# Sixteen row slots instead of nine in the gathers of two graph convolutions

## The chip, the cores and the metric

The kernel runs on one core of a Trainium2 chip. The time is the device time of one execution in microseconds (us). Before the change the median of three timed runs is 11113.99 us (11105.82 to 11126.48).

## The reference, cut to what matters

The kernel computes four layers of a graph network over 6250 nodes of 128 features and 106250 edges (100000 edges and one loop for each node), sorted by destination. The last layer is two graph convolutions, and the change touches these alone:

```
def _graph_conv(h, src, dst, Wr, br, Ws, ew=None):
    m = h[src]
    if ew is not None:
        m = m * ew[:, None]
    agg = jax.ops.segment_sum(m, dst, num_segments=h.shape[0])
    return agg @ Wr + br + h @ Ws
h = relu(_graph_conv(x, src, dst, Wr0, br0, Ws0, edge_weight))
h = relu(_graph_conv(h, src, dst, Wr1, br1, Ws1))
return _layernorm(x + h)
```

## The kernel before, in words

The kernel is a sequence of stages with a barrier of all engines between any two. First the edges are sorted by source and by destination; then come the attention layers, each of which gathers node rows by edge; then `gather_conv` runs twice (lines 2650 and 2653), once from `x_table` to `conv_table` ("conv0") and once from `conv_table` to the output ("conv1").

The edges, padded, are cut into tiles of 128 and the tiles into `R` = 126 groups of `G` = 7. Only 879 of the 882 tiles hold edges. For each group the engines of `gather_conv` do the following, in program order on each engine, with semaphores between them:

- GpSimd (line 1426 on) issues one indirect DMA a tile. It fetches the 128 rows (512 bytes each) that the tile's edges name from the table in HBM into `rows[:, g % deep, t % G, :]`. `deep` is the number of row slots, 9 before the change, each of seven tiles. Each slot has a semaphore `fetched[g % deep]`. Before the first gather of a group `g >= deep` GpSimd waits until the group that used the slot before has been multiplied.
- VectorE builds `weighted_hot(g + 1)` (line 1460): for each tile a 128x128 matrix that has an edge's weight in the column of its destination, counted from the tile's first destination. There are `near` = 3 buffers. Then, in `add(g)`, it waits for `summed >= g + 1` and adds the group's seven 128x128 products from PSUM to `acc` and `odd` by turns (line 1473), at an offset that it loads from a table.
- TensorE's `sums(g)` waits for the hot matrices, for the slot's rows and for a free PSUM buffer (`near` = 3 of these too). It then multiplies rows by hot matrix, seven products that appear in the profile as 14 weight loads and 14 matmuls since they are f32 (line 1526), and the last one increments `summed`. Every nine groups it also transposes four blocks of the layer's own input and multiplies them by `Ws` (lines 1534, 1542, 1543); ScalarE copies these out of PSUM (lines 1388, 1392). Once the sums of a block of nodes are complete, which is the case only in the last groups (118 on), it is multiplied by `Wr` (lines 1555, 1556) and finished on VectorE and ScalarE.
- ScalarE in conv0 also issues a small DMA a group (line 1419), which nothing on the other engines waits for within the stage.

The wait that the change moves, and the only one on GpSimd in this stage:

```
for g in range(R):
    if g >= deep:
        pool.wait_ge(summed, g - deep + 1)
    for t in range(g * G, min(g * G + G, TD)):
        pool.indirect_dma_start(
            rows[:, g % deep, t % G, :], None, table, ...).then_inc(fetched[g % deep], 16)
```

The attention stages (`attend`, gathers at line 1644) have the same loop with `RING` = 19 slots, and there the slot is freed by a later step (`msg_ready`, or `summed`).

Of the kernel before, what the change touches and what calls it, by code (L numbers as in the profile page):

```python
# [1340 lines left out]
                    pipelined(pe, R // SLOTS, SLOTS, differences, sums)  # L1341


def gather_conv(nc, c, o, name, acc, alpha, table, k, unit=None, deep=9, near=3):

# [1219 lines left out]
def gnn_kernel(nc, out, x_in, src, dst, length, edge_weight, real, p):  # L2567
    with ExitStack() as keep:
# [18 lines left out]
        with ExitStack() as first_layer:  # L2587
# [4 lines left out]
            with ExitStack() as sums:  # L2592
                scores = sums.enter_context(nc.sbuf_tensor("scores", [P, T * H0], F32))
                with ExitStack() as edges:
# [53 lines left out]
        h_nodes = sb("h_nodes", [P, NB, D])  # L2648
        unit = sb("unit", [P, T])
        gather_conv(nc, c, by_dst, "conv0", acc, by_dst.weight, x_table,  # L2650
                    {"own": x, "wr": conv_w[:, 0], "ws": conv_w[:, 1], "b": conv_b[0:1, 0], "nodes": h_nodes,
                     "table": conv_table}, unit)
        gather_conv(nc, c, by_dst, "conv1", acc, unit, conv_table,
                    {"own": h_nodes, "wr": conv_w[:, 2], "ws": conv_w[:, 3], "b": conv_b[0:1, 1], "nodes": h_nodes,
                     "residual": x, "out": out})
# [43 lines left out]
```

## Time and profile before

| | |
|---|---|
| Median of the timed runs | 11113.99 us |
| The profiled execution's own time | 11120.83 us |
| Its span | 11119.1 us |
| GpSimd busy | 6028.3 us (54%) |
| TensorE matmuls busy | 5741.4 us (52%) |
| VectorE busy | 5139.9 us (46%) |
| ScalarE busy | 2208.4 us (20%) |
| Mean granted TensorE clock | 0.638 of full speed |
| Gathers of conv0 | 8492.9 to 9745.0 us |
| Gathers of conv1 | 9790.4 to 11041.8 us |

PE is TensorE, PEld its weight loads, DVE is VectorE, ACT is ScalarE, POOL is GpSimd, SP is SyncE. In a timeline each row gives the start in us from the span's beginning, the duration, the engine, the line, the instruction with what it writes and reads, how many such instructions were merged into the row, and in brackets how long the engine was idle before it and what ended that idle time. That last name is inferred; where it is a DMA that had long landed, another semaphore ended the wait. "issue" is time in which the engine waited for nothing that the profile shows. No engine is busy for much more than half of the span, so the time is set by waits between them, stage by stage.

### The profile page before, as it was taken

How to read it: one execution, taken by the hardware profiler on the slowest of the kernel's cores; microseconds unless marked ns; L12 is line 12 of the kernel's file. 1: busy time of each engine (PE TensorE's matmuls, PEld its weight loads, DVE VectorE, ACT ScalarE, POOL GpSimd, SP SyncE). 2: the span in 40 equal slices, each digit the busy share in tenths (PEclk: the TensorE clock that was granted, in tenths of full speed). 3: DMA queues.
4: the chain of work that ended last, by engine and by line, in shares of the span. 5: the costliest groups of instructions: out<-in, count | busy, mean ns of one | idle time of the engine just before them, and what ended most of it. 6: DMA issues, size and time to landing. Idle time of an engine off the chain costs nothing. (4 is left out here: it accounts for less than half of the span.)

```text
span 11119.1 us, 123007 instructions
## 1 busy us (share of the span) xinstructions
PE 5741.4 (52%) x32437; PEld 5060.6 (46%) x32437; DVE 5139.9 (46%) x16751; ACT 2208.4 (20%) x4780; POOL 6028.3 (54%) x6231
## 2 busy tenths in 40 slices
PE   6656654566635666653555554466562333333333
PEld 5545544566634555543455543355452333233323
DVE  7555543333356666662555554244454333333334
ACT  0111111111114444431433433211111000000000
POOL 2555554555534666644544442465543666656664
PEclk8555556777765666666777776555555556666656
DMA  1000004555533444423333333233321222221111
GB/s 28 9 9 10 9 1 116 159 160 159 162 85 92 105 105 105 101 84 86 95 92 93 95 90 40 58 66 65 65 52 32 47 47 47 47 51 46 47 46 46
DMA packets 991728, 792.42 MB, mean 71 GB/s; under 512 B 425142, under 2 KB 866874, under 8 KB 991024
## 3 DMA queue, kind: packets, MB, share of 16 engines
q1 hardware_dynamic: 535572, 373.20, 13.4%
q0 software_dynamic: 211104, 354.07, 13.3%
q10 hardware_dynamic: 244600, 60.13, 2.5%
q8 instruction: 160, 2.62, 0.1%
q14 instruction: 292, 2.39, 0.1%
HBM read 692.16 MB, written 94.60 MB: 71 GB/s over the span
## 5 line engine op out<-in xcount | busy, mean ns | idle before, releaser
L1526 PE MATMUL conv_ps_sum<-conv_hot,conv_rows 128*128 128x128 f32 x3528 | 729.2, 382 | 1523.2 <-DVE conv_hot L1460 1034.7
L1526 PEld LDWEIGHTS conv_ps_sum<-conv_hot,conv_rows 128*128 128x128 f32 x3528 | 665.5, 285 | 1585.6 <-DVE conv_hot L1460 1119.6
L515 POOL DMA_INDIRECT payload_src<-load_src_pay,load_src_at_i x879 | 897.7, 1021 | 804.7 <-DVE load_src_at_i L479 543.2
L1644 POOL DMA_INDIRECT attend_rows<-xl_table,dst_other x879 | 829.7, 944 | 871.3 <-DVE attend_msg L1876 592.4
L1051 POOL DMA_INDIRECT scores_rows<-kv_table,scores_idx x882 | 834.0, 946 | 661.6 <-DVE scores_prod L1125 330.5
L1431 POOL DMA_INDIRECT conv_rows<-x_table,dst_other x879 | 840.6, 956 | 626.7 <-issue 252.8
L636 POOL DMA_INDIRECT payload_dst<-place_dst_pay,place_dst_at_i x879 | 855.8, 974 | 589.5 <-DVE place_dst_at_i L777 314.5
L1644 POOL DMA_INDIRECT attend_rows<-h_table,dst_other x879 | 830.7, 945 | 619.7 <-issue 236.0
L1431 POOL DMA_INDIRECT conv_rows<-conv_table,dst_other x879 | 840.0, 956 | 456.7 <-issue 254.9
L1473 DVE TENSOR_TENSOR acc<-acc,conv_ps_sum 128x128 f32 x1008 | 291.4, 289 | 1687.7 <-DMA x_table<-x_nodes 771.4
L1704 PE MATMUL attend_ps_x<-attend_win,attend_hot_t 128*128 128x136 f32 (+1 forms) x3528 | 754.1, 321 | 408.9 <-issue 226.9
L1704 PEld LDWEIGHTS attend_ps_x<-attend_win,attend_hot_t 128*128 128x128 f32 x3528 | 658.0, 257 | 464.3 <-issue 437.5
L1721 PE MATMUL attend_ps_sum<-attend_hot,attend_rows 128*128 128x128 f32 x1764 | 417.3, 429 | 505.3 <-DVE acc L1896 465.3
L1085 PE MATMUL scores_ps_len<-const_ident,scores_length 128*128 128x128 f32 x1764 | 383.9, 403 | 518.5 <-ACT scores_hidden L1030 295.6
L1721 PEld LDWEIGHTS attend_ps_sum<-attend_hot,attend_rows 128*128 128x128 f32 x1764 | 385.4, 330 | 521.9 <-issue 521.9
L1896 DVE TENSOR_TENSOR acc<-acc,attend_ps_sum 128x128 f32 x1764 | 505.5, 287 | 234.9 <-remote 67.6
L1721 PE MATMUL attend_ps_sum<-attend_hot,attend_msg 128*128 128x128 f32 x1764 | 343.2, 360 | 519.3 <-DVE acc L1896 415.9
L1085 PEld LDWEIGHTS scores_ps_len<-const_ident,scores_length 128*128 128x128 f32 x1764 | 353.8, 305 | 537.4 <-issue 537.4
L1721 PEld LDWEIGHTS attend_ps_sum<-attend_hot,attend_msg 128*128 128x128 f32 x1764 | 303.3, 261 | 560.2 <-issue 513.3
L1790 ACT ACTIVATE attend_hot_t<-attend_rel_all,const_minus_lane 128x896 f32<-128x896 bf16 x252 | 261.5, 1038 | 1303.7 <-remote 724.8
L1841 DVE SCALAR_TENSOR_TENSOR attend_mix<-attend_ps_x,att_wide 128x408 f32<-128x408 f32 x378 | 181.7, 484 | 722.6 <-remote 597.2
L691 PE MATMUL place_dst_ps_look<-place_dst_tab,place_dst_lo_t 128*128 128x50 f32 x1764 | 335.8, 367 | 304.8 <-DVE place_dst_picked L771 282.7
(442 smaller groups left out, 14393.1 us busy)
## 6 DMA issues: line engine op xcount, KB each, us to landing
attend_win<-xr_table SPq DMA_DIRECT2D x882, 68.0 KB
scores_win<-q_table ACTq DMA_DIRECT2D x882, 64.0 KB
spill<-scores_rows SPq DMA_DIRECT2D x126, 448.0 KB
place_dst_key_all<-key_rows_dst SPq DMA_DIRECT2D x126, 448.0 KB
place_dst_rows<-spill SPq DMA_DIRECT2D x126, 448.0 KB
attend_rel_all<-rel_flat_dst SPq DMA_DIRECT2D x252, 224.0 KB
place_dst_low_all<-low_rows_dst SPq DMA_DIRECT2D x126, 224.0 KB
scores_rows<-kv_table,scores_idx POOLq DMA_INDIRECT x882
```

What stands on the lines that cost most here:

```text
L515: pool.indirect_dma_start(o.payload, bass.IndirectOffsetOnAxis(ap=at_i[:, t:t + 1].bitcast(U32), axis=0), pay[:, t, :], None).then_inc(sca ...
L636: pool.indirect_dma_start(o.payload, bass.IndirectOffsetOnAxis(ap=at_i[:, t:t + 1].bitcast(U32), axis=0), pay[:, t, :], None).then_inc(sca ...
L691: mm = pe.matmul(ps_look[:, j, 0:HB], lo_t[:, g % 2, j, :], tab[:, g % 2, j, :], start=True, stop=True)
L1051: pool.indirect_dma_start(rows[:, s, j, :], None, table, bass.IndirectOffsetOnAxis(ap=idx[:, s, j:j + 1].bitcast(U32), axis=0)).then_inc(g ...
L1085: mm = pe.matmul(ps_len[:, j, :], length[:, s, j:j + 1].to_broadcast([P, P]), c.ident[:], start=True, stop=True)
L1431: pool.indirect_dma_start(rows[:, g % deep, t % G, :], None, table, bass.IndirectOffsetOnAxis(ap=o.other[:, t:t + 1].bitcast(U32), axis=0) ...
L1473: dve.tensor_tensor(at, at, ps_sum[:, n, j, :], ALU.add).then_inc(added, 1)
L1526: mm = pe.matmul(ps_sum[:, g % near, j, :], rows[:, g % deep, j, :], hot[:, g % near, j, :], start=True, stop=True)
L1644: pool.indirect_dma_start(rows[:, g % RING, t % G, :], None, table, bass.IndirectOffsetOnAxis(ap=o.other[:, t:t + 1].bitcast(U32), axis=0) ...
L1704: mm = pe.matmul(ps_x[:, bank, at:at + window_w], hot_t[:, g % 2, j, :], win[:, g % 3, j, :], start=True, stop=not two_sided)
L1721: mm = pe.matmul(ps_sum[:, j, :], what, hot[:, g % 2, j, :], start=True, stop=True)
L1896: dve.tensor_tensor(at, at, ps_sum[:, j, :], ALU.add).then_inc(added, 1)
```

## The change

One default value is changed. Both calls use it, so both convolutions have sixteen slots of seven tiles. The tile `rows` grows from 9 x 7 x 128 f32 (32,256 bytes a partition) to 16 x 7 x 128 f32 (57,344 bytes), and there are sixteen `fetched` semaphores instead of nine. `near`, the number of hot matrices and of PSUM buffers, stays 3.

```
-def gather_conv(nc, c, o, name, acc, alpha, table, k, unit=None, deep=9, near=3):
+def gather_conv(nc, c, o, name, acc, alpha, table, k, unit=None, deep=16, near=3):
```

## Rows read from the trace of the kernel before

**Rows 1.** The gathers' own line: durations, and what GpSimd's idle time before them ended with.

```profile
L1431 POOL DMA_INDIRECT conv_rows<-x_table,dst_other x879: 938/944/7480, 8492.9 to 9745.0; - x176
L1431 POOL DMA_INDIRECT conv_rows<-conv_table,dst_other x879: 938/944/7480, 9790.4 to 11041.8; - x176
...
  DMA x_table<-x_nodes: 155.7, 51
  DMA attend_rows<-h_table,dst_other: 153.3, 54
  PE conv_ps_sum L1526: 8.2, 4
```

**Rows 2.** Timeline of GpSimd, first convolution: start, duration, instruction, idle before.

```profile
8492.92 0.94 POOL L1431 DMA_INDIRECT conv_rows<-x_table,dst_other  x1 [214.15 <-POOLq L78]
...
8515.83 0.94 POOL L1431 DMA_INDIRECT conv_rows<-x_table,dst_other  x1 [0.30 <-issue]
...
8594.52 0.94 POOL L1431 DMA_INDIRECT conv_rows<-x_table,dst_other  x1 [0.30 <-issue]
8602.42 0.94 POOL L1431 DMA_INDIRECT conv_rows<-x_table,dst_other  x1 [6.95 <-DMA x_table<-x_nodes]
...
9104.77 0.94 POOL L1431 DMA_INDIRECT conv_rows<-x_table,dst_other  x1 [3.86 <-DMA x_table<-x_nodes]
...
9134.65 0.94 POOL L1431 DMA_INDIRECT conv_rows<-x_table,dst_other  x1 [3.86 <-DMA x_table<-x_nodes]
...
9745.04 0.94 POOL L1431 DMA_INDIRECT conv_rows<-x_table,dst_other  x1 [0.30 <-issue]
```

**Rows 3.** Timeline of TensorE, the second, third and fourth groups of the first convolution.

```profile
8518.44 3.33 PE L1526 MATMUL conv_ps_sum<-conv_hot,conv_rows 128*128 128x128 f32 x14 [4.84 <-DMA conv_rows<-x_table,dst_other]
...
8527.27 3.23 PE L1526 MATMUL conv_ps_sum<-conv_hot,conv_rows 128*128 128x128 f32 x14
...
8551.07 0.37 PE L1526 MATMUL conv_ps_sum<-conv_hot,conv_rows 128*128 128x128 f32 x1 [2.43 <-issue]
8553.87 0.37 PE L1526 MATMUL conv_ps_sum<-conv_hot,conv_rows 128*128 128x128 f32 x1 [2.43 <-issue]
```

**Rows 4.** Timeline of VectorE, the first additions of some groups of the first convolution.

```profile
8602.28 0.29 DVE L1473 TENSOR_TENSOR acc<-acc,conv_ps_sum 128x128 f32 x1 [75.76 <-DMA x_table<-x_nodes]
...
8616.38 0.29 DVE L1473 TENSOR_TENSOR acc<-acc,conv_ps_sum 128x128 f32 x1 [10.76 <-DMA x_table<-x_nodes]
...
9104.63 0.29 DVE L1473 TENSOR_TENSOR acc<-acc,conv_ps_sum 128x128 f32 x1 [19.10 <-DMA x_table<-x_nodes]
...
9134.51 0.29 DVE L1473 TENSOR_TENSOR acc<-acc,conv_ps_sum 128x128 f32 x1 [17.75 <-DMA x_table<-x_nodes]
...
9748.22 0.29 DVE L1473 TENSOR_TENSOR acc<-acc,conv_ps_sum 128x128 f32 x1 [3.79 <-PE conv_ps_sum L1526]
...
9751.47 0.28 DVE L1473 TENSOR_TENSOR acc<-acc,conv_ps_sum 128x128 f32 x1
...
9779.39 0.29 DVE L1473 TENSOR_TENSOR acc<-acc,conv_ps_sum 128x128 f32 x1 [0.97 <-PE conv_ps_sum L1526]
```

**Rows 5.** Timeline of ScalarE, then two stretches of the first convolution (columns as headed).

```profile
8563.68 0.59 ACT L1392 COPY h_nodes<-conv_ps_n 128x512 f32<-128x512 f32 x1 [49.46 <-DMA attend_rows<-h_table,dst_other]
...
core 0: us, PE busy (x) PEld busy (x) DVE busy (x) ACT busy (x) POOL busy (x), PEclk, DMA share, GB/s
8493.00:8596.00 103.00, 20.37 (x76) 17.26 (x76) 21.05 (x44) 1.17 (x2) 79.30 (x77) 0.53 0.20 49
9104.00:9134.00 30.00, 15.41 (x57) 12.60 (x57) 10.05 (x42) 0.58 (x1) 19.92 (x21) 0.56 0.22 47
```

**Rows 6.** Two stretches of the first attention stage, and GpSimd's timeline in it.

```profile
5045.00:5095.00 50.00, 4.33 (x16) 3.72 (x16) 2.03 (x3) 2.08 (x2) 37.74 (x40) 0.50 0.31 70
5195.00:5245.00 50.00, 33.34 (x243) 31.53 (x242) 32.97 (x78) 21.43 (x27) 0.00 (x0) 0.91 0.60 139
...
5254.43 0.94 POOL L1644 DMA_INDIRECT attend_rows<-xl_table,dst_other  x1 [93.54 <-DVE attend_msg L1876]
```

## The prediction

> **What bounds the kernel now.** I read the page's head first, then its costliest groups, then the gathers' own line, the engines' timelines at the start, middle and end of the first convolution, and a table of stretches. The change touches only the two convolution stages at the end, each with 879 gathers. The reader is to see two things in the gathers' rows. One gather occupies GpSimd for 944 ns, and the next starts 0.30 us later, so the steady pace is 1.25 us a gather and 8.75 us a group of seven (8492.92 to 8594.52 is 76 steps, one of which is the 7.48 us of the longest gather). At that pace 879 gathers are 1098 us, but the first convolution's run from 8492.9 to 9745.0, which is 1252 us; the second's is the same to a microsecond [rows 1, 2]. The difference is GpSimd standing still: 155.7 + 153.3 + 8.2 = 317 us over both stages, in 109 waits [rows 1]. The first two names in those rows are DMAs that had long ended; by the code the only thing a gather waits for here is `summed` of the group that held its slot, so these are waits for a free slot, and they are what more slots could take away.
>
> Who is late? Not the gathered data. Group 1's last gather starts at 8515.83 and its matmuls start at 8518.44: 2.6 us from issue to use, against nine slots that cover 79 us [rows 2, 3]. The late one is the consumer, in a peculiar way. The third group's matmuls stand at 8527.27 and take 3.23 us, yet VectorE, which waits for nothing but their semaphore, starts that group's additions at 8602.28, after 75.76 us idle [rows 3, 4]. Meanwhile TensorE's rows crawl: the last two matmuls of the fourth group start at 8551.07 and 8553.87, 2.80 us apart with one weight load between them, so 1.40 us an instruction, where the group before took 3.23 / 14 = 0.23 us for such a pair [rows 3]. ScalarE gets the semaphore of the products that ended at 8527 only at 8563.68 [rows 5]. From there to VectorE's release at 8602.28 is 38.6 us, and a group is 28 TensorE instructions: 28 x 1.40 = 39.2 us. So while GpSimd issues gathers without a break, TensorE's work goes through at about 39 us a group, far slower than GpSimd's 8.75 us, and GpSimd runs to the end of its slots: 77 gathers, eleven groups, before its first stop [rows 2, 5].
>
> In the middle the same thing repeats with a period of some 30 us. GpSimd stands still for 3.86 us (to 9104.77), then again to 9134.65; between them are 21 gathers, three groups. VectorE's additions come in bursts right at those moments (9104.63 after 19.10 us idle, 9134.51 after 17.75 us idle) [rows 2, 4, 5]. The pause of GpSimd is what lets the consumer catch up by three groups, and the slot it hands back lets GpSimd go on. Over the stage the consumer goes from group 2 (8602.28) to group 118 (9748.22): 1145.9 / 116 = 9.88 us a group. Once GpSimd is done (9746) and quiet, it takes 3.25 us for an ordinary group (9748.22 to 9751.47) [rows 2, 4].
>
> **The change, part by part.** *Instructions.* None is added or removed: 879 gathers, 126 groups, the same matmuls. Seven more semaphores and 25,088 bytes more a partition cost nothing that a row shows; I put them at 0, with the stage's set-up (the 5 us or so before its first memset) as the upper end.
>
> *The start of a convolution.* GpSimd needs `summed` of group g-16 instead of g-9. Groups 0 to 15 wait for nothing, 16, 17 and 18 need the first, second and third sum, which are there by 8602. Group 19 needs the fourth. By the crawl of 39 us a group this comes at 8602 + 39 = 8641, and the fifth at 8680, and GpSimd reaches groups 19 and 20 at 8493 + 6.5 (the long gather) + 19 x 8.75 = 8666 and 8674. So the first stop moves from before group 11 to before group 19 or 20. The price is the shift, less what the crawl got done in it: 8 x 8.75 - 1 x 9.88 = 60.1 us, or 9 x 8.75 - 2 x 9.88 = 59.0 us. I take 59.5 us. The bounds: 0 if the crawl is not caused by GpSimd's run and the consumer would have gone free at 8602 anyway; 79 us if nothing at all goes through in the longer run.
>
> *The middle.* The cycle of three groups and a pause depends on where the consumer stands relative to its own semaphores, not on how far ahead the slot is that it frees: the data has landed 2.6 us after issue in either case. So 9.88 us a group stays. This is the term I can prove least.
>
> *The end.* When the last gather is issued, the consumer is behind by up to sixteen groups instead of nine. Seven more groups are therefore consumed in quiet, at 3.25 to 3.4 us and not 9.88: (9.88 - 3.35) x 7 = 45.7 us gained. The lower bound is 38 us, at the pace of the last seven groups, which also carry the closing products: (9779.39 - 9748.22) / 7 = 4.45 us [rows 4].
>
> *Sum.* 59.5 - 45.7 = +13.8 us a convolution, +28 us for two (ends of the terms: 2 x (0 - 45.7) = -91 to 2 x (79 - 38) = +82). On the profiled execution's own 11120.8 us (span 11119.1) this is 11149. The median of the timed runs is 6.8 us lower, so 11142.
>
> There is a second case of a long run with more slots in this trace: the first attention stage has 19, and it is the same form of gather. It starts at 4995; in 5045 to 5095 GpSimd issues 40 gathers while TensorE gets 16 matmuls done; GpSimd then stands still for 93.54 us until 5254.43, and in 5195 to 5245, with no gather, TensorE does 243 [rows 6]. A longer ring there bought a longer starved run and a longer stop.
>
> **The rule that speaks the other way.** The trace shows the same gap of 3.9 us over and over on GpSimd [rows 2]. The Trainium skill, page "Perfetto Trace Analysis", section "Optimization Strategy", says that consistent bubbles on the engine that should be saturated can mean that there isn't enough SBUF for the next tile (number of buffers). By that rule the change is the cure, and the time is that of rival 2 below; the trace agrees that the wait is for a slot, but not that the slots are few against the 2.6 us of a landing.
>
> **Rivals.** (1) *The start does not get dearer.* If the crawl ends by itself at about 8602, and the pause of GpSimd has only the same moment, the 59.5 us disappear and the 45.7 us at the end stay: 11120.8 - 91 = 11029, or 11023 on the median. For it: ScalarE's semaphore came at 8563.68 and VectorE's at 8602.28, inside or just after an unbroken run, and 39.2 us predicts the second without any pause. Against it: the same arithmetic gives the next group another 39 us, and the additions of group 3 came at 8616.38, right after a second pause [rows 4]. It decides from the point at which less than 45.7 of the 59.5 us are lost.
> (2) *The slots do what they are for.* Without any stop, 317 us go; if sixteen groups are left at the end, 7 x 3.35 x 2 = 47 us come back: 11120.8 - 317 + 47 = 10851. Against it is the consumer's 9.88 us against GpSimd's 8.75.
> (3) *It cancels.* The start costs 40 to 50 us, as when the longer run lets one or two groups more slip through: 11100 to 11130, no change.
>
> **How the numbers follow.** A measurement of this kernel can tell about 0.2% (22 us) from no change. Forecast, the start outweighs the end: 0.50, with its own range 11125 to 11175. Rival 3: 0.26. Rival 1: 0.19. Rival 2: 0.05. The forecast case lies mostly above 11136, a tenth of it below, and rival 3 has a small upper tail that makes up for this, so slower is 0.50, same 0.26, faster 0.24. The range reaches from 11040, into the milder half of rival 1, up to 11180.
>
> **What would show it.** In the changed profile: the first row of a gather with an idle time of several us in the first convolution comes after 133 to 140 gathers instead of 77, and VectorE's idle row of 76 us is followed by rows of 20 to 39 us before that stop. In the middle the pauses keep a period near 30 us with 21 gathers. The gathers' waits sum to some 295 us instead of 317, and from the last gather to the last addition it is 55 to 60 us instead of 34. Wrong is the forecast if the additions after 8602 go on at 10 us a group while GpSimd still has free slots, or if the pauses vanish.

## The result, and the profile after

The changed kernel takes 11140.14 us (median of 9 runs, 11126.24 to 11170.75) where the kernel before takes 11108.96 us on the same chip (9 runs, 11098.13 to 11140.3). The ratio is 1.0034 with an interval of 1.0022 to 1.0046: slower by 31 us. The forecast was 11142 us, slower by 28. The profiled execution of the changed kernel has 11149.92 us (span 11148.2).

Times within a convolution are given below from its first gather. This table is worked out from the timelines of both kernels. "Sum of group n" is the first of VectorE's additions of that group, and the tail is from the start of the last gather to the first addition of the last group, 125.

| us from the first gather | before, conv. 1 | after, conv. 1 | before, conv. 2 | after, conv. 2 |
|---|---|---|---|---|
| sum of group 2 | 109.4 | 106.0 | 109.4 | 108.7 |
| sum of group 3 | 123.5 | 145.2 | 123.5 | 147.9 |
| sum of group 4 | 126.7 | 184.4 | 126.7 | 187.1 |
| sum of group 5 | 131.6 | 211.7 | 130.8 | 211.6 |
| sum of group 10 | 193.2 | 255.0 | 193.1 | 254.6 |
| sum of group 60 | 678.9 | 747.2 | 691.1 | 746.8 |
| sum of group 100 | 1083.1 | 1147.1 | 1089.4 | 1151.4 |
| start of the last gather | 1252.1 | 1250.7 | 1251.4 | 1251.4 |
| sum of group 125 | 1286.5 | 1306.3 | 1310.2 | 1331.3 |
| tail | 34.3 | 55.6 | 58.7 | 80.0 |

The gathers' own line after the change, against [rows 1]:

```profile
L1431 POOL DMA_INDIRECT conv_rows<-x_table,dst_other x879: 942/947/7470, 8480.9 to 9731.6; - x176
L1431 POOL DMA_INDIRECT conv_rows<-conv_table,dst_other x879: 942/947/7470, 9798.2 to 11049.6; - x176
...
  DMA attend_rows<-h_table,dst_other: 152.9, 46
  DMA attend_rel<-rel_rows_dst: 152.5, 42
```

From the first gather to the last it is 1250.7 and 1251.4 us, as before (1252.1 and 1251.4). GpSimd still stands still for 152.9 + 152.5 = 305 us, and not 317. The waits are fewer and longer. GpSimd's timeline, first convolution, against [rows 2]:

```profile
8665.42 0.95 POOL L1431 DMA_INDIRECT conv_rows<-x_table,dst_other  x1 [2.86 <-DMA attend_rows<-h_table,dst_other]
...
8692.73 0.95 POOL L1431 DMA_INDIRECT conv_rows<-x_table,dst_other  x1 [18.80 <-DMA attend_rows<-h_table,dst_other]
...
9081.17 0.95 POOL L1431 DMA_INDIRECT conv_rows<-x_table,dst_other  x1 [4.18 <-DMA attend_rows<-h_table,dst_other]
...
9111.22 0.95 POOL L1431 DMA_INDIRECT conv_rows<-x_table,dst_other  x1 [4.01 <-DMA attend_rows<-h_table,dst_other]
...
9731.59 0.95 POOL L1431 DMA_INDIRECT conv_rows<-x_table,dst_other  x1 [0.30 <-issue]
```

The first stop is now before gather 141, the first of group 20. Before, it was before gather 78. The second, one group later, is 18.80 us. In the middle the old cycle is back: 30.05 us between two stops of some 4 us. VectorE's additions at the start, against [rows 4]:

```profile
8586.88 0.29 DVE L1473 TENSOR_TENSOR acc<-acc,conv_ps_sum 128x128 f32 x1 [73.48 <-DMA attend_rows<-h_table,dst_other]
...
8626.08 0.29 DVE L1473 TENSOR_TENSOR acc<-acc,conv_ps_sum 128x128 f32 x1 [35.85 <-DMA attend_rows<-h_table,dst_other]
...
8665.28 0.29 DVE L1473 TENSOR_TENSOR acc<-acc,conv_ps_sum 128x128 f32 x1 [35.85 <-DMA attend_rows<-h_table,dst_other]
...
8692.59 0.29 DVE L1473 TENSOR_TENSOR acc<-acc,conv_ps_sum 128x128 f32 x1 [23.96 <-DMA attend_rows<-h_table,dst_other]
```

These are the sums of groups 2, 3, 4 and 5. The first three are 39.20 us apart, twice. The kernel before had only the first of these idle rows: its next sum came 14.10 us later, during GpSimd's second stop, and the one after it 3.3 us after that. TensorE's timeline in the same time shows what crawls:

```profile
8590.28 3.36 PE L1526 MATMUL conv_ps_sum<-conv_hot,conv_rows 128*128 128x128 f32 x14 [52.14 <-issue]
8629.48 3.36 PE L1526 MATMUL conv_ps_sum<-conv_hot,conv_rows 128*128 128x128 f32 x14 [35.84 <-DVE conv_hot L1460]
```

The row at 8590.28 is the fifth lot of fourteen, group 4. Once it is started it takes 3.36 us, against 3.33 and 3.23 us in [rows 3], and is done at 8593.64; VectorE adds its products at 8665.28, 72 us later. So the multiplications themselves are not slow here. What comes late is the semaphore that tells of them, and TensorE then idles because VectorE can't hand it the next hot matrices and PSUM buffer. "Crawl" below means this: the sums of one group after another reach VectorE some 39 us apart. ScalarE's first copy against [rows 5], and four stretches (start and end, length, then busy time and count of TensorE's products, its weight loads, VectorE, ScalarE and GpSimd, the granted clock, the DMA share, GB/s):

```profile
8547.58 0.59 ACT L1392 COPY h_nodes<-conv_ps_n 128x512 f32<-128x512 f32 x1 [45.05 <-issue]
```

```profile
8481.00:8584.00 103.00, 20.40 (x76) 17.21 (x76) 21.05 (x44) 1.17 (x2) 79.58 (x77) 0.53 0.20 49
8584.00:8660.00 76.00, 6.72 (x28) 6.13 (x28) 6.69 (x28) 0.00 (x0) 57.65 (x61) 0.52 0.21 53
8481.00:9732.00 1251.00, 402.32 (x1818) 353.16 (x1818) 383.86 (x1569) 14.82 (x26) 841.62 (x879) 0.59 0.22 47
9732.00:9794.00 62.00, 49.51 (x396) 47.70 (x396) 54.34 (x211) 7.75 (x13) 0.54 (x1) 0.93 0.29 50
```

The first 103 us are those of before to the last count (76 products, 77 gathers). Then come 76 us of the longer run that the further slots bought: 61 gathers issued, and 28 products done. In the 62 us after the last gather there are 396 products. The same two stretches of the kernel before, on GpSimd's stretch and on what followed it:

```profile
8493.00:9746.00 1253.00, 423.86 (x1927) 373.03 (x1928) 408.04 (x1668) 14.79 (x26) 840.47 (x879) 0.60 0.23 47
9746.00:9786.00 40.00, 34.92 (x289) 34.43 (x288) 31.05 (x111) 7.56 (x12) 0.00 (x0) 0.88 0.34 75
```

In the same time of GpSimd, TensorE got 1927 - 1818 = 109 products fewer done. They moved behind the last gather. That is the effect: the producer takes as long as before, and the consumer is further behind when it ends.

To the start of the last group's additions this is 1306.3 - 1286.5 = 19.8 us in the first convolution and 1331.3 - 1310.2 = 21.1 us in the second, 41 us together. The profiled executions differ by 29 us only, because the stages ahead of the first convolution, which the change doesn't touch, took 12.0 us less in the changed kernel's (its first gather is at 8480.9, and was at 8492.9).

### The profile page after: what moved, and what is told of

It is laid out like the page before. It is cut to its first block and busy times, and to the rows that moved or that the text cites. A ratio compares the mean times of both kernels' runs of the same rounds, so it can differ in the third digit from the quotient of the medians.

```text
span 11148.2 us, 123007 instructions
## 1 busy us (share of the span) xinstructions
PE 5717.2 (51%) x32437; PEld 5039.4 (45%) x32437; DVE 5139.5 (46%) x16751; ACT 2211.5 (20%) x4780; POOL 6046.2 (54%) x6231
```

## The experiments

Two theories stood against each other. **Theory A** is that of the prediction: while GpSimd issues gathers without a break, TensorE's work goes through at 39 us a group, more slots mean a longer unbroken run, and the catching up at the end gives back only a part. **Theory B** is plain buffering: fewer slots make GpSimd stop longer, so fewer than nine must be slower. A third view was tested beside them, that only the start of a stage crawls.

The kernel before was run beside each experiment, and it turned out that the chips are of two kinds. On three of those with experiments ("e5", "e10" and "e12"), and in the runs of the result, whose chip is one of these or a fourth, it takes 11106 to 11121 us. On three others (the rest of the experiments) it takes 8840 to 8845 us, and there TensorE never crawls. That was not known when the first four were forecast, and none of the outcomes forecast for those four under either theory came. Nine runs in all fell on chips without the crawl and tell something other than what they were meant for.

**The changed kernel again.** No edit: `deep=16` as in the change.

> The changed kernel itself, beside the kernel before on one chip. In the four comparisons made so far here (three, five, late sixteen slots, and the pause) the kernel before took 8840 us and not 11114, and GpSimd never waited for a slot. If the kernel before is again at 8840, theory A expects no difference (ratio 1.000, within 0.002): without TensorE's crawl the consumer keeps up with 8.8 us a group, no slot is ever waited for, and sixteen slots stand as empty as nine. If it is again near 11110, theory A expects the ratio on record, 1.003, with the first stop of GpSimd before group 20. Rival: sixteen slots cost something by themselves (memory placement, semaphores), and the ratio is 1.003 at 8840 too.

Measured: 11163.02 us against 11105.91; the ratio is 1.005, from 1.0034 to 1.0065. The sums come at 110.8, 150.0, 188.5 and 211.7 us in the first convolution, the last gather starts at 1249.8 and the tail is 55.3 us. VectorE's timeline:

```profile
8648.69 0.29 DVE L1473 TENSOR_TENSOR acc<-acc,conv_ps_sum 128x128 f32 x1 [35.86 <-DMA attend_rows<-h_table,dst_other]
...
8687.19 0.29 DVE L1473 TENSOR_TENSOR acc<-acc,conv_ps_sum 128x128 f32 x1 [35.16 <-DMA attend_rows<-h_table,dst_other]
```

The slowdown (forecast 1.003) and its shape come again in a second set of runs, with the first stop before group 20; the step here is 39.2 and then 38.5 us.

**Fewer slots, and more of them later, on chips without the crawl.** Three and five slots change one number:

```diff
-def gather_conv(nc, c, o, name, acc, alpha, table, k, unit=None, deep=9, near=3):
+def gather_conv(nc, c, o, name, acc, alpha, table, k, unit=None, deep=3, near=3):
```

```diff
-def gather_conv(nc, c, o, name, acc, alpha, table, k, unit=None, deep=9, near=3):
+def gather_conv(nc, c, o, name, acc, alpha, table, k, unit=None, deep=5, near=3):
```

> Three row slots instead of nine in both convolutions, nothing else. Theory A (GpSimd's unbroken run starves TensorE, which gets a group through in 39.2 us while it lasts; what the run costs at the start is partly paid back at the end): the first stop comes before group 5 and not 11, some 52 us earlier, and at the end six groups fewer are consumed in quiet, 6 x 6.6 = 40 us lost. So about 12 us less a convolution, 25 us less in all than before (ratio 0.998). TensorE's crawl at the start shrinks from 76 us to about 25. Theory B (slots are plain buffering): with 26 us of slots GpSimd stops more often and longer, its waits grow over the 317 us of before, and the kernel is 50 us or more slower.

> Five row slots instead of nine. Theory A: first stop before group 7, 35 us earlier; four groups fewer in quiet at the end, 26 us lost; 9 us less a convolution, 17 us less in all (ratio 0.9985). Theory B: slower than before, between the three slots and the nine.

> Three row slots again, to be read if the kernel before is near 11110 here, that is where TensorE crawls. Theory A (an unbroken run of GpSimd starves TensorE, 39.2 us a group; slots let the run at the start grow and are paid back in part at the end): sizes from nine against sixteen are 66 us lost at the start and 48 us won back at the end for seven slots, so six slots fewer save 57 and cost 41 us: 16 us less a convolution, 25 to 32 us less in all (ratio 0.9975). The first stop of GpSimd comes before group 5. Theory B (plain buffering): the slots cover 26 us against a consumer that is served in bursts of 30 us, so GpSimd's stops grow well over 159 us a convolution and the kernel is 50 us or more slower. If the kernel before is at 8840: same.

The late widening has the changed kernel's sixteen slots, but GpSimd stays within nine groups of the consumer up to group 59:

```diff
-                    if g >= deep:
-                        pool.wait_ge(summed, g - deep + 1)
+                    back = 9 if g < 60 else deep
+                    if g >= back:
+                        pool.wait_ge(summed, g - back + 1)
```

> Sixteen slots are there, but up to group 59 GpSimd waits as with nine, and from group 60 as with sixteen. Theory A: the starved run doesn't belong to the start but to any unbroken run of GpSimd; it comes at group 60, seven groups and more without a stop, costs about the same 60 to 66 us there and pays back 46 to 48 us at the end, so the time is that of sixteen slots from the start, 28 to 38 us over before. Rival (only the cold start of the stage starves TensorE): nothing is lost at group 60 and the end pays back 46 us a convolution, so 90 us less than before.

> Sixteen slots, used as nine up to group 59, where the kernel before is near 11110. Theory A: an unbroken run of nine or more groups from group 60 with the third, fourth, fifth sum 39.2 us apart, a loss of 60 to 66 us there and 48 us won back at the end: 28 to 57 us over before in all (ratio 1.0025 to 1.005), as with sixteen from the start. Rival (only the stage's start can starve): 90 us less than before (0.992). If the kernel before is at 8840: same.

Measured: three slots 8836.36 us against 8839.9 (ratio 0.9999, 0.999 to 1.0008), and again 8845.67 against 8845.17 (1.0002, 0.9993 to 1.0011); five slots 8837.73 against 8839.9 (1.0000, 0.9991 to 1.0009); the late widening 8835.57 against 8839.9 (0.9999, 0.999 to 1.0008), and again 8843.92 against 8845.17 (0.9997, 0.9988 to 1.0006). Five runs of three kernels, and none can be told from nine slots. The gathers' own line with three slots says why:

```profile
L1431 POOL DMA_INDIRECT conv_rows<-x_table,dst_other x879: 940/944/7477, 6574.1 to 7678.9; - x176
L1431 POOL DMA_INDIRECT conv_rows<-conv_table,dst_other x879: 938/944/7486, 7696.2 to 8801.3; - x176
its engine sat idle before it (us, times) until:
  issue: 535.1, 1756
  POOLq L78: 212.4, 2
```

There is no wait for a slot at all, with three slots. The last gather starts 1104.8 us after the first, and 878 x 1.25 + 6.5 for the one long gather is 1104. So nothing that the kernel computes needs nine slots, let alone sixteen. One stretch of the first convolution and one of the first attention stage, and VectorE's first addition of group 2, of the same kernel:

```profile
6574.00:6677.00 103.00, 39.64 (x164) 35.67 (x164) 48.72 (x156) 1.76 (x3) 79.60 (x77) 0.58 0.25 49
4057.00:4107.00 50.00, 26.99 (x167) 25.84 (x166) 18.91 (x35) 12.50 (x12) 37.81 (x41) 0.81 0.59 147
```

```profile
6611.85 0.29 DVE L1473 TENSOR_TENSOR acc<-acc,conv_ps_sum 128x128 f32 x1 [5.08 <-PE conv_ps_sum L1526]
```

77 gathers in 103 us, as in [rows 5], but 164 products beside them where the crawling chip did 76. In the attention stage it is 167 products beside 41 gathers in 50 us, against 16 beside 40 in [rows 6]. The third sum comes at 37.7 us and not at 109.4. GpSimd's pace and the 49 GB/s of the DMAs are the same on both kinds. The gathers' unbroken issue is thus not enough to make TensorE crawl; something that differs between the chips belongs to it. These five runs don't tell A from B: on these chips neither has anything to act on.

**A pause of GpSimd ahead of every third group.** If GpSimd's silence is what lets TensorE go on, short early pauses should pay for themselves. GpSimd waits until the gathers of the group before have landed:

```diff
+                    if g and g % 3 == 0:
+                        pool.wait_ge(fetched[(g - 1) % deep], landed(g - 1, deep))
```

> Nine slots as before, and before every third group GpSimd waits until its own last gathers have landed (about 2.2 us after their issue). Theory A, with the pause as what frees TensorE: the crawl never builds up or ends at each pause, the consumer keeps up, and GpSimd's own pace sets the time: 1098 us of issue + 42 pauses of 1.5 to 2.5 us = 1160 to 1200 us instead of 1252, with a short tail; 60 to 100 us less a convolution, 120 to 200 us less in all. If a landing is too short a pause to free TensorE (the stops in the trace lasted 3.9 us): no better than before, or up to 2 x 42 x 1.6 = 130 us slower. Theory B (TensorE's crawl has nothing to do with GpSimd's run): GpSimd has slack of 154 us a convolution, so the pauses change nothing: same as before.

> Nine slots, and before every third group GpSimd waits for its own last landing; where the kernel before took 8840 us this pause was 2.36 us each and the kernel 167 us slower. Where the kernel before is near 11110: if a silence of 2.4 us frees TensorE (theory A with a short release), the crawl never lasts over 26 us, the consumer keeps up, and 60 to 100 us a convolution are saved, ratio 0.982 to 0.99. If TensorE needs the 3.9 us of silence that ended each crawl in the trace, the pauses add to or replace the stops: 0.998 to 1.01. If the crawl has nothing to do with GpSimd's issuing, the pauses eat only its slack of 159 us a convolution: 1.000.

> The pause before every third group once more, to be read if the kernel before is near 11110. If a silence of 2.4 us frees TensorE (theory A with a short release): 60 to 100 us saved a convolution, ratio 0.982 to 0.99. If TensorE needs some 3.9 us of silence, as ended each crawl in the trace: 0.998 to 1.01. If the crawl has nothing to do with GpSimd's issuing, the pauses (42 of 2.36 us, 99 us a convolution) only eat its slack of 159 us: 1.000. If the kernel before is at 8840: 1.019 as twice before.

> The pause before every third group, to be read if the kernel before is near 11110. GpSimd's stops so far come every three or four groups and last 3.9 us whatever the slots, as if 26 us of issue and 3.9 us of silence were one cycle. If a silence of 2.4 us, put there every 26 us, frees TensorE as well: no further stops, GpSimd is done after 1098 + 42 x 2.4 = 1199 us instead of 1252, and the consumer is at most four groups behind: 60 to 100 us saved a convolution, ratio 0.982 to 0.99. If it takes the 3.9 us: the pauses are too short, stops come on top of them, 0.998 to 1.01. If the crawl has nothing to do with GpSimd's issuing: 1.000. If the kernel before is near 8840: 1.019.

Measured: 9007.04 us against 8839.9 (1.0196, 1.0182 to 1.021), 9012.93 against 8845.17 (1.0192, 1.0178 to 1.0206), 9004.08 against 8843.22 (1.0185, 1.0168 to 1.0202) and 9011.63 against 8844.36 (1.0185, 1.0167 to 1.0203). It fell on a chip without the crawl each time, four times in all. The first of them is slower than every outcome forecast for it. From it the price was known, and 1.019 was forecast for such a chip in two of the later ones. What it shows is the price of the pauses where they bring nothing, in the waits of the gathers' line:

```profile
  DMA conv_rows<-conv_table,dst_other: 94.6, 41
  DMA conv_rows<-x_table,dst_other: 94.5, 40
```

94.5 / 40 = 2.36 us each, where a gap of 0.30 us would have stood anyway: 41 x 2.06 = 84 us a convolution, and twice that is about the 167 us of the medians. Whether 2.4 us of silence frees TensorE on a crawling chip was not seen and stays open.

**The late widening on a crawling chip.** The same edit as above. It tells whether the loss belongs to the start of a stage or to any unbroken run.

> Sixteen slots used as nine up to group 59, once more, to be read if the kernel before is near 11110. Theory A: GpSimd runs on from group 60 for nine groups or more without a stop, and in that run the sums come 39.2 us apart; 60 to 66 us lost there a convolution, 48 us won back at the end, 28 to 57 us over before (ratio 1.0025 to 1.005). Rival (only a stage's start starves TensorE): 90 us less than before (0.992). If the kernel before is near 8840: 1.000.

Measured: 11151.14 us against 11109.12, ratio 1.0035 (1.002 to 1.0049). The start is that of nine slots: the sums of groups 2 to 5 come at 110.1, 123.5, 126.8 and 130.9 us, where the kernel before has 109.4, 123.5, 126.7 and 131.6. The loss comes where the slots come. GpSimd's timeline around group 60; the rows between the first two all have 0.30 us of idle time:

```profile
9067.52 0.95 POOL L1432 DMA_INDIRECT conv_rows<-x_table,dst_other  x1 [3.98 <-DMA attend_rows<-h_table,dst_other]
...
9177.85 0.94 POOL L1432 DMA_INDIRECT conv_rows<-x_table,dst_other  x1 [5.47 <-DMA attend_rows<-h_table,dst_other]
...
9195.46 0.95 POOL L1432 DMA_INDIRECT conv_rows<-x_table,dst_other  x1 [9.15 <-DMA attend_rows<-h_table,dst_other]
```

VectorE's in the same time, and its first addition of the last group:

```profile
9100.70 0.29 DVE L1474 TENSOR_TENSOR acc<-acc,conv_ps_sum 128x128 f32 x1 [21.19 <-DMA attend_rows<-h_table,dst_other]
...
9139.20 0.29 DVE L1474 TENSOR_TENSOR acc<-acc,conv_ps_sum 128x128 f32 x1 [35.15 <-DMA attend_rows<-h_table,dst_other]
...
9177.71 0.29 DVE L1474 TENSOR_TENSOR acc<-acc,conv_ps_sum 128x128 f32 x1 [35.17 <-DMA attend_rows<-h_table,dst_other]
...
9791.03 0.29 DVE L1474 TENSOR_TENSOR acc<-acc,conv_ps_sum 128x128 f32 x1 [0.97 <-PE conv_ps_sum L1527]
```

At the widening GpSimd runs for 110.3 us and twelve groups without a stop, and the sums come 38.5 us apart as at a start with sixteen slots. From group 60 on the kernel stands where the changed one stands: the sum of group 60 at 748.3 us (747.2), of group 100 at 1146.6 (1147.1), of group 125 at 1305.3 (1306.3). The loss belongs to the longer unbroken run wherever it falls, not to the start of the stage. Nor does it come from the larger tile or the seven further semaphores as such: they are there from the start in this kernel, and up to group 59 it keeps the pace of nine slots.

**Five slots on a crawling chip.** If A holds, the opposite edit must win: GpSimd stops earlier, and less is left for the tail.

> Five row slots once more, to be read if the kernel before is near 11110. In the profiles of nine, sixteen and late sixteen slots GpSimd's own stretch from first to last gather is 1250 to 1252 us whatever the slots, and only the tail after it changes: 34 us with nine, 55 to 57 us with sixteen. Theory A: GpSimd's stretch stays 1250 us (first stop before group 7, cycle of 30 us unchanged), and the tail is four groups shorter, some 4 x 2.9 = 12 us; 8 to 13 us saved a convolution, 16 to 26 us in all (ratio 0.9977 to 0.9986). Theory B (plain buffering): GpSimd's stretch grows by 10 us or more. If the kernel before is near 8840: 1.000.

Measured: 11099.45 us against 11121.01, ratio 0.9977 (0.9962 to 0.9991): faster than nine slots, and so than both kernels of this case. The gathers' own line:

```profile
L1431 POOL DMA_INDIRECT conv_rows<-x_table,dst_other x879: 938/944/7476, 8493.4 to 9743.7; - x176
L1431 POOL DMA_INDIRECT conv_rows<-conv_table,dst_other x879: 938/944/7478, 9781.3 to 11033.6; - x176
...
  DMA attend_rows<-h_table,dst_other: 314.4, 134
```

Its GpSimd at the start of the first convolution:

```profile
8568.09 0.94 POOL L1431 DMA_INDIRECT conv_rows<-x_table,dst_other  x1 [7.18 <-DMA attend_rows<-h_table,dst_other]
...
8597.86 0.94 POOL L1431 DMA_INDIRECT conv_rows<-x_table,dst_other  x1 [3.83 <-DMA attend_rows<-h_table,dst_other]
```

And VectorE at the first of these, and at the last group:

```profile
8567.96 0.29 DVE L1473 TENSOR_TENSOR acc<-acc,conv_ps_sum 128x128 f32 x1 [40.70 <-DMA attend_rows<-h_table,dst_other]
...
9770.31 0.29 DVE L1473 TENSOR_TENSOR acc<-acc,conv_ps_sum 128x128 f32 x1 [0.97 <-PE conv_ps_sum L1526]
```

The first row is the sum of group 2, at 74.5 us. With nine and with sixteen slots it came at 106 to 111 us in every trace of a crawling chip. What the edit changes up to there is that GpSimd fell silent, at 8560.9, and 7 us later the sum was there. This is the direct evidence that GpSimd's silence lets TensorE's work through.

The slots side by side, first convolution on crawling chips, from the timelines:

| slots | first gather to last | stops over 0.6 us, sum | sum of group 100 | tail | sum of group 125 |
|---|---|---|---|---|---|
| 5 | 1250.3 | 159.3 | 1050.0 | 26.6 | 1276.9 |
| 9 | 1252.1 | 159.2 | 1083.1 | 34.3 | 1286.5 |
| 16 | 1250.7 | 154.8 | 1147.1 | 55.6 | 1306.3 |
| 16 from group 60 | 1250.0 | 155.9 | 1146.6 | 55.4 | 1305.3 |

The first two columns hardly move; the tail does. Both convolutions together are 9.6 + 12.3 = 22 us shorter with five slots (medians: 21.6) and 18.8 + 20.5 = 39 us longer with the late sixteen (medians: 42.0). Theory B falls.

## Why the prediction came out as it did

**The bound and its mechanism: right, on this kind of chip.** The consumer is late, not the data: three slots are enough where TensorE is not slowed. That GpSimd's run slows TensorE's work is shown by five slots, where a stop 35 us earlier brought the third sum 35 us earlier, and by the late widening. The premise "while GpSimd issues without a break, TensorE crawls" was put too generally, though. On three of the six chips of the experiments GpSimd issues for 1105 us without a break and TensorE keeps up. And "TensorE's rows crawl" holds only for the last matmuls of the fourth group in [rows 3]. In the steps of 39.2 us a group's matmuls take 3.36 us, and it is their semaphore that comes late. The sum isn't touched by this, since it goes by the additions of VectorE.

**The start of a convolution: right in its steps, too low in its sum.** The first stop was forecast before group 19 or 20 and is before group 20. The sums forecast for 8641 and 8680 came at 8626.08 and 8665.28; the rate of 39.2 us is exact, and everything lies 15 us earlier, 12.0 of which is the earlier first gather. The term was 59.5 us. Measured against the kernel before it is 80.1 us at the sum of group 5, 61.8 at group 10, 68.3 at group 60 and 64.0 at group 100, so about 64 at the place that counts. What I had not seen is the length of the second stop. In the kernel before it was this row, and during it the sums of groups 3 and 4 came through:

```profile
8616.52 0.94 POOL L1431 DMA_INDIRECT conv_rows<-x_table,dst_other  x1 [5.60 <-DMA x_table<-x_nodes]
```

With sixteen slots GpSimd stood for 18.80 us (16.0 in the second convolution) until the sums of groups 5 and 6 came. The first stop freed nothing in either kernel: with nine slots the sum of group 2 came at 109.4 us, no earlier than the 106.0 to 110.8 us of sixteen slots without any silence. With five slots 7 us of silence were enough. Why it took longer with sixteen isn't shown.

**The middle: right.** The period is 30.05 us between two stops (forecast near 30), and from the sum of group 10 to that of group 100 it is (1147.1 - 255.0) / 90 = 9.91 us a group, against (1083.1 - 193.2) / 90 = 9.89 before. This was the term I called least provable.

**The end: right.** 45.7 us were to be won back; from group 100 on, 64.0 - 19.8 = 44.2 are, in the first convolution. The tail was forecast at 55 to 60 us and is 55.6. In the second convolution it is 62.0 - 21.1 = 40.9, with a tail of 80.0 us, 58.7 before. The waits sum to 305 us; forecast were some 295. The long second stop can account for the difference, but no run separates it.

**The sum.** +13.8 us a convolution was forecast, +19.8 and +21.1 are measured. In the first convolution the mis-sized term is the start, by 4.5 us at group 100, and the end by 1.5 us. In the second it is the other way round: the start is 1151.4 - 1089.4 = 62.0 us, 2.5 over, and the end 4.8 us short. The forecast of the whole time is nearer than its terms deserve: 41 us are lost in the convolutions, and the unrelated 12 us of the earlier stages lie against them in the profiled execution. By the medians the loss is 31 us in the first runs and 57 us in the second, around the 41. That the first median lies within 2 us of the forecast is luck.

A simpler sum would have been closer. The loop of GpSimd and its consumer runs at 9.9 us a group whatever the slots, so the last gather is issued at the same moment, with seven more groups behind it. These cost the quiet pace: 7 x 3.25 = 23 us a convolution by [rows 4], measured 19.8 and 21.1.

**The rivals.** Rival 1 (the start does not get dearer) fell with the sums 39.2 us apart after that of group 2, rival 3 with the ratio and its interval. Rival 2, that the slots do what they are for, is refuted most plainly: the Trainium skill, page "Perfetto Trace Analysis", section "Optimization Strategy", takes consistent bubbles on the engine that should be saturated as a possible sign of too few buffers. Here GpSimd's bubbles were indeed waits for a slot, and the sum of its stops in the first convolution is 159.3, 159.2 and 154.8 us with five, nine and sixteen.

**What stays open.** What on some chips holds TensorE's semaphores back to the pace of 1.40 us an instruction while GpSimd issues gathers; the traces name no resource. Whether the recording of the profile has a part in it isn't tested, since every run's time here comes with a recorded span and clock. That GpSimd's stretch stays at 1249 to 1252 us with five, nine and sixteen slots is measured, not explained. How long a silence frees them, and why the second stop took 18.80 us, stay open too. Three slots and the pauses were not seen on a crawling chip.

## What to carry to other kernels

A wait for a free slot says that somebody is late, not that slots are few. Compare the time from issue to use (2.6 us here) with the lead that the slots allow (79 us): if the lead is already far larger, the consumer is late, and more slots only let the producer run further ahead, which is paid after its last transfer. Take such a small change to more than one chip, because here the two kinds of chip disagree on whether there is a wait at all.

## What the runs showed of the hardware that was not expected

- The same kernel takes 11106 to 11121 us on three chips and in the runs of the result, and 8840 to 8845 us on three others: 20% less, far more than any edit here. Most of it lies in the seven stages with indirect gathers: from first gather to last they take 2155 us more in the profile of the kernel before than in that of three slots, of 2284 us between the two spans. A convolution's run from the first gather to the last is 1249 to 1252 us on the one kind and 1105 to 1107 us on the other.
- On the first kind the sums reach VectorE 38.5 to 39.2 us apart during unbroken gathers, that is 1.40 us for each of a group's 28 TensorE instructions (estimate from the 2.80 us between the last matmuls in [rows 3]), though the fourteen matmuls themselves take 3.36 us. The steps were 39.2 or 38.5 us in the result and on two chips of the experiments, in the middle of a stage as at its start.
- On the first kind GpSimd's run over 879 gathers is 1249 to 1252 us with five, nine and sixteen slots; by the terms of the forecast it would have been 1242 with sixteen (1252 + 59.5 - 7 x 9.88).
- The granted clock in the 62 us after the last gather is 0.93, over the whole run of gathers 0.59. The slow stretch of 76 us has 0.52, about the lower level of 1.2 GHz, with 28 products in it.
